# Pyramid-pooled attention on one core: earlier weights, turns of the identity, another order in the last batch, and six banks for the last projections

## The reference, cut to what matters

```python
# x: (8, 512, 64, 64) f32; qk_w: (256, 512); v_w: (512, 512); out_w: (512, 512)
qk  = relu(bn(einsum('bchw,oc->bohw', x, qk_w)))
val = relu(bn(einsum('bchw,oc->bohw', x, v_w)))
key    = psp(qk)                        # max pools to 1, 3x3, 6x6, 8x8: 110 cells
value  = psp(val).transpose(0, 2, 1)
query  = qk.reshape(B, 256, H * W).transpose(0, 2, 1)
scores = softmax(einsum('bnc,bcs->bns', query, key) * 256 ** -0.5)
y = einsum('bns,bsc->bnc', scores, value)      # back to (B, 512, H, W)
return x + bn(einsum('bchw,oc->bohw', y, out_w))
```

## Time and profile before

| what | value |
|---|---|
| median of 3 runs | 1314.9 us (1314.38 to 1315.77) |
| profiled execution, its own time | 1314.11 us |
| its span | 1312.4 us |
| TensorE busy | 1283.3 us, 98% of the span |
| GpSimd, VectorE, ScalarE busy | 951.9, 947.3, 688.7 us |
| granted clock of TensorE over the span | 0.997 |

### The profile page before, as it was taken

The page is one execution under the profiler, slowest core; times in us unless marked ns, Lnnn a source line. Parts: engine busy times, 40 slices in busy tenths (PEclk is TensorE's granted clock), DMA queues, the critical chain, the costliest instruction groups (busy, mean ns, idle before and its releaser), DMA issues.

```text
span 1312.4 us, 16789 instructions
## 1 busy us (share of the span) xinstructions
PE 1283.3 (98%) x5539; PEld 1036.1 (79%) x5539; DVE 947.3 (72%) x2171; ACT 688.7 (52%) x1017; POOL 951.9 (73%) x414
## 2 busy tenths in 40 slices
PE   7999999999999999999999999999999999999996
PEld 6777788887888878887888877888788887888875
DVE  6555677777777778778777777777867778876466
ACT  5333555644555654555654465654555647754421
POOL 1888988877878867887777786877778826765522
PEclk9999999999999999999999999999999999999998
DMA  6323356566676656676556676666667669995226
GB/s 225 113 97 113 112 177 213 196 217 223 210 240 217 198 187 232 211 238 224 182 207 232 222 232 204 205 200 233 206 219 239 211 205 365 331 308 201 96 97 257
DMA packets 134538, 272.20 MB, mean 207 GB/s; under 512 B 9227, under 2 KB 9267, under 8 KB 134451
## 3 DMA queue, kind: packets, MB, share of 16 engines
q1 hardware_dynamic: 133874, 270.07, 60.9%
q10 hardware_dynamic: 576, 1.05, 0.2%
HBM read 174.61 MB, written 96.47 MB: 207 GB/s over the span
## 4 chain that ended last, share of the span: by engine, by line
PE 79%; DVE 7%; POOL 7%; ACT 3%; DMA 2%; issue 2%; SPq 0%; DVEq 0%; ACTq 0%; POOLq 0%
PE conv_ps L690 16%; PE conv_ps L688 16%; PE conv_ps L692 16%; POOL xl L578 5%; PE out_ps L772 4%; PE out_ps L773 3%; PE out_ps L774 3%; PE conv_ps L673 3%; PE conv_ps L674 3%; PE conv_ps L672 3%; PE score_ps L746 2%; PE score_ps L745 2%; PE score_ps L747 2%; DVE row_max L1336 1%; DMA xa<-x 1%
## 5 line engine op out<-in xcount | busy, mean ns | idle before, releaser
L1336 DVE TENSOR_REDUCE row_max<-conv_ps 128x64 f32<-128x384 f32 (+2 forms) x576 | 284.5, 530 | 149.0 <-ACT q_out L1035 68.2
L578 POOL TENSOR_TENSOR xl<-xa,xh 128x1024 fp32r<-128x1024 f32 x108 | 258.0, 2418 | 84.5 <-ACT xh L964 84.5
L688 PE MATMUL conv_ps<-xh,sh 128*128 128x512 f32 x648 | 253.5, 391 | 3.8 <-POOL xl L578 1.8
L690 PE MATMUL conv_ps<-xh,sl 128*128 128x512 f32 x648 | 254.3, 393 | 0.0
L692 PE MATMUL conv_ps<-xl,sh 128*128 128x512 f32 x648 | 254.3, 392 | 0.0
L578 POOL TENSOR_TENSOR xl<-tt,xh 128x1024 fp32r<-128x1024 f32 x81 | 194.3, 2415 | 10.2 <-ACT xh L964 10.2
L688 PE MATMUL conv_ps<-xh,wh 128*128 128x512 f32 x486 | 190.2, 391 | 4.1 <-POOL xl L578 2.7
L692 PE MATMUL conv_ps<-xl,wh 128*128 128x512 f32 x486 | 190.7, 392 | 0.0
L690 PE MATMUL conv_ps<-xh,wl 128*128 128x512 f32 x486 | 190.6, 392 | 0.0
L972 ACT ACTIVATE conv_ps<-conv_ps 128x512 f32<-128x512 f32 x81 | 47.2, 583 | 253.6 <-PE conv_ps L692 252.9
L1476 DVE SCALAR_TENSOR_TENSOR xo<-out_ps,shift,xo 128x512 f32<-128x512 f32 x205 | 151.9, 745 | 34.5 <-DMA xo<-x 18.0
(11 more groups left out here) (227 smaller groups left out, 2527.7 us busy)
## 6 DMA issues: line engine op xcount, KB each, us to landing
xa<-x SPq DMA_DIRECT2D x148, 512.0 KB, 5.5
xo<-x SPq DMA_DIRECT2D x104, 512.0 KB, 4.3
out<-xo SPq DMA_DIRECT2D x104, 512.0 KB, 3.7
queries<-q_out SPq DMA_DIRECT2D x112, 256.0 KB, 2.5
q_in<-queries SPq DMA_DIRECT2D x50, 512.0 KB, 4.1
tt<-x SPq DMA_DIRECT2D x13, 512.0 KB, 5.5
out<-tt SPq DMA_DIRECT2D x13, 512.0 KB, 4.9
early<-queries SPq DMA_DIRECT2D x6, 512.0 KB, 7.8
```

The costliest lines, as they stand in the source:

```text
L578: nc.gpsimd.tensor_tensor(xl[:, b0:b1, :], raw, xh[:, b0:b1, :], ALU.subtract).then_inc(x_lo, 1)
L688: nc.tensor.matmul(out[:, :], hi[:, k, :], xh[:, b + k, :], start=first, stop=False, skip_group_check=True)
L690: nc.tensor.matmul(out[:, :], lo[:, k, :], xh[:, b + k, :], start=False, stop=False, skip_group_check=True)
L1336: last = nc.vector.tensor_reduce(row_max[:, c, n, :], src[:, r0_ * W:r1_ * W].rearrange("p (r w) -> p w r", w=W), AX.X, ALU.max)
```

## The change

The parts of the diff below belong to three places.

At the start: SyncE's queue gets the value weights 1 and 3 behind the two halves of x and before the key weights, ScalarE's queue keeps weights 0 and 2, and SyncE no longer waits before tile 1 of x. `scale_weights(1)` stands before the first split of x on VectorE. `keep_busy(n)` turns the identity n times into `conv_ps[2]`, whose content nothing reads: 5 times before the turn of the batch norm rows, 7 behind it, 10 between the first two turned weights and `conv(0, 0)`.

In the last image's values (s = 65 to 70): `scores(s - 8)` stands before `conv(s, 0)` instead of behind `conv(s, 1)`, and `sums(s - 8)` stands behind `conv(s, 1)` in the same s, where before it opened s + 1. GpSimd, ScalarE and VectorE follow: `split_q_lo` before `split_lo`, `exps` and `split_q_hi` before `split_hi`, `split_e_lo` before the pooling, `refine` and `normalise` before the pooling of group 2 and `split_p_lo` behind it.

At the very end: six banks in turn for the 32 projections, and nothing of tile 62's softmax is left there; tile 63's `sums` comes one tile earlier.

```diff
+        LAST_BANKS = [out_ps[0], *conv_ps[0:3], out_ps[1], score_ps]
         def out_bank(a, m):
-            return [out_ps[0], *conv_ps[0:3]][m] if a >= LAST else out_ps[m % 2]
+            return LAST_BANKS[(OC * (a - LAST) + m) % len(LAST_BANKS)] if a >= LAST else out_ps[m % 2]
@@ sync
+            for m in ORDER[2:VC]:
+                sp.dma_start(w_raw(m), v_w[m * P:(m + 1) * P, :]).then_inc(w_in[m], 16)
             sp.dma_start(qk_raw[:, :, :], qk_w.rearrange("(m p) c -> p m c", p=P)).then_inc(w_in[VC], 16)
-            sp.wait_ge(w_in[VC - 1], 16)
             load(1)
@@ gpsimd
-                if LAST < s < S:
+                if s < X - 1 and s not in (LAST, S):
                     split_q_lo(s - (NT - 1))
...
-                if s < X - 1 and not LAST < s < S:
+                if s in (LAST, S):
                     split_q_lo(s - (NT - 1))
@@ tensor
+            def keep_busy(n):
+                for _ in range(n):
+                    nc.tensor.transpose(conv_ps[2][:, 0:P], ident[:, :], ident[:, :])
             pe.wait_ge(ident_made, 2)
+            keep_busy(5)
             pe.wait_ge(bn_in, 16)
             nc.tensor.transpose(conv_ps[3][:, 0:4 * PAR], bn_rows[:, :], ident[0:4 * PAR, 0:4 * PAR]).then_inc(bn_turned, 1)
@@ project
-                if copied(a - 1, m):
-                    pe.wait_ge(y_copied, a - LAST)
-                else:
-                    wait(pe, out_added, added(a - 1, m) if a > LAST else OC * a + m - 1)
+                n = OC * (a - LAST) + m
+                if n >= len(LAST_BANKS):
+                    n -= len(LAST_BANKS)
+                    if copied(LAST + n // OC, n % OC):
+                        pe.wait_ge(y_copied, n // OC + 1)
+                    else:
+                        pe.wait_ge(out_added, added(LAST + n // OC, n % OC))
+                elif n < 0:
+                    wait(pe, out_added, OC * a + m - 1)
+                elif n == 0:
+                    pe.wait_ge(out_added, OC * LAST - 1)
+                elif n == 5:
+                    pe.wait_ge(p_lo, S - 1)
@@ tensor
+            keep_busy(7)
             turn_weights(0)
             turn_weights(1)
+            keep_busy(10)
...
             for s in range(S, X):
-                if s < X - 1:
+                if s <= S + 1:
                     sums(ap)
                 if s == S:
                     project(ap - 1, 2)
                     project(ap - 1, 3)
+                elif s < X - 1:
+                    scores(ac)
                 conv(s, 0)
                 conv(s, 1)
                 if s == S:
                     project(ap, 0)
                     project(ap, 1)
                 elif s < X - 1:
-                    scores(ac)
+                    sums(ac)
                 conv(s, 2)
...
-            sums(S - 2)
             for a in range(LAST, S):
                 for m in range(OC):
                     project(a, m)
-                if a == LAST + 2:
+                if a == LAST + 1:
                     sums(S - 1)
@@ scalar
-            for m in ORDER[0:VC]:
+            for m in ORDER[0:2]:
                 act.dma_start(w_raw(m), v_w[m * P:(m + 1) * P, :]).then_inc(w_in[m], 16)
...
+            for s in range(S + 1, X - 1):
+                a = s - NT
+                if s == S + 1:
+                    guess(a - 1)
+                exps(a)
+                split_q_hi(a + 1)
+                split_hi(s + 1, 0)
+                split_hi(s + 1, 1)
+                if s == S + 1:
+                    split_p_hi(a - 1)
+                guess(a)
+                split_p_hi(a)
...
             exps(S - 1)
-            guess(S - 2)
             copy_out(LAST)
-            split_p_hi(S - 2)
@@ vector
+            scale_weights(1)
             split_first_lo(0)
             weights_lo(0)
-            scale_weights(1)
             split_first_lo(1)
...
+                    if s < X - 1:
+                        split_e_lo(ac)
...
                 for c in range(VC):
+                    if c == 2 and S < s < X - 1:
+                        refine(ac)
+                        normalise(ac)
                     pool_tile_rows(s, c)
+                    if c == 2 and S < s < X - 1:
+                        split_p_lo(ac)
...
             add_outs(LAST)
             split_e_lo(S - 1)
-            refine(S - 2)
             add_outs(LAST + 1)
-            normalise(S - 2)
             add_outs(LAST + 2)
-            split_p_lo(S - 2)
+            refine(S - 1)
             add_outs(LAST + 3)
-            refine(S - 1)
             normalise(S - 1)
```

More of the change, by code:

```diff
@@ L1184, in _ @@
                 store_pair_q(s, 3)
-            for s in range(LAST, X):
+            for s in range(LAST, S + 1):
                 ap, ac = s - NT - 1, s - NT
-                if 0 <= ap < S - 2:
-                    guess(ap)
+                guess(ap)
                 if s == LAST + 1:
@@ L1200, in _ @@
                     split_q_hi(ac + 1)
-                if s + 1 < X:
-                    split_hi(s + 1, 0)
+                split_hi(s + 1, 0)
                 if s == LAST:
                     split_hi(s + 1, 1)
-                if 0 <= ap < S - 2:
-                    split_p_hi(ap)
+                split_p_hi(ap)
                 if s == LAST:
@@ L1211, in _ @@
                     finish_keys(ac // NT)
-                if LAST < s < X - 1:
+                if LAST < s:
                     split_hi(s + 1, 1)
@@ L1222, in _ @@
                     continue
-                if 0 <= ac < S - 1 and not LAST < s < S:
+                if s == S:
                     exps(ac)
-                if 0 <= ac + 1 < S and not LAST < s < S:
                     split_q_hi(ac + 1)
@@ L1676, in _ @@
                         add_out(ap, 2 * c - 1)
-                    if c == 2 and s < X - 1:
+                    if c == 2 and s == S:
                         split_e_lo(ac)
```

## The result

The changed kernel takes 1304.62 us (median of 4 runs, 1303.7 to 1305.68); the kernel before, measured with it, 1315.13 us (1314.38 to 1315.77). The ratio is 0.9921, with a 95% interval of 0.9905 to 0.9937: 10.5 us less. The profiled execution of the change took 1303.70 us, with a span of 1302.0 us.

A forecast was written before the change was run, and what follows sets the result against it. TensorE, busy 98% of the span, bounds the kernel; start -2.4 and tail -8.0 give -10.4 on 1314.1, 1303.7, plus 0.8 for the median: 1304.5 us. Range: about 1302.6, with 0.7 for the runs' spread, to 1308.2.

The forecast's parts named there:

- The start: Up to the first convolution's end: earlier scaling, reordered loads and turns gain 2.4 us, all kept to the end.
- the rise of the clock: TensorE at the start: upper clock level reached at 10.6 us at the latest, at the earliest by the convolution's start.
- The rule against the change: First convolution: by the skill's rule transposes do not bring the full clock, so the turns would not raise it.
- rival B: First convolution: turns do not raise the clock, only its own matmuls do; gain 0.7 instead of 2.4, 1306.2 us; chance 0.27.
- The last image: Last image's values: moved sums cost 0.5 us and one new wait for queries 0.3 us, 0.8 in all.
- The end: Last projections and stores: TensorE goes through without a stop, then stores bind at 373 GB/s; 8.8 us gained before subtracting 0.8.
- My other two estimates of this term: Span's end: 1304.5 by the old lag behind the last add, 1304.9 by the worse window's 353 GB/s, against 1303.6 taken.
- One of my own signs of being wrong: Projections over 26 us, stores more than 6 us behind the adds, or new waits in tiles 65 to 70.
- my sum of 22.9 us for the projections: Tail: the 32 projections and last sums, 98 matmuls, need 22.9 us at 0.234 us spacing, against 30.9 before.
- C: Tail: VectorE or the copies on ScalarE and GpSimd set the pace; 2.8 us missing, 1307.3 us; chance 0.14.
- D: Start: loads of one queue share bandwidth, second half of x lands near 14.5 us; 1310.6 us; chance 0.05.
- E: Tiles 65 to 70: TensorE waits in each for the queries' low part; slower, 1317.5 us or more; chance 0.03.

The follow-up runs named there:

- run 2: The changed kernel with loads, order of weight scaling and turns at the start as before, last image and end as in the change: 1307.87 us, ratio 0.9945.
- run 3: The changed kernel with four banks and the old waits for the last projections, as before: 1307.43 us, ratio 0.994.
- run 5: The changed kernel storing only the second half of the channels of tiles 56 to 62, output incomplete: 1301.81 us, ratio 0.9891.
- runs 3 and 4: Besides run 3, the kernel before with five banks in turn for the last projections and nothing else: 1312.12 us, ratio 0.9975.
- run 1: The changed kernel without its 22 turns of the identity: 1306.56 us, ratio 0.9939.
- run 9: The changed kernel with the second weight scaled behind the first low weight, as before: 1308.2 us, ratio 0.9947.
- run 6: The changed kernel with the last image stored in quarters of a tile, each as soon as it is added: 1303.57 us, ratio 0.9913.
- run 12: The changed kernel itself once more, for a second profile: 1304.87 us, ratio 0.9928.
- run 10: The changed kernel without the group of ten turns; the groups of 5 and 7 stay: 1306.58 us, ratio 0.9929.
- run 8: The changed kernel with all four value weights on ScalarE's queue and SyncE waiting for the last, as before: 1305.42 us, ratio 0.9928.
- run 7: The changed kernel with quarter-tile stores and low parts of the second and third combined weights made while tile 1 is pooled: 1304.15 us, ratio 0.9916.

## Why the prediction was right

The sum was -10.4 us on the profiled execution, and -10.4 was measured; the forecast of 1304.5 stands against 1304.62. The mechanisms were right, but that the number is met so closely is luck. Two of its terms were off and cancelled; the stretch between them, which differs among executions by up to 4.4 us, happened to be almost as long in both profiles (1166.5 and 1166.1 us).

*The start* was put at 2.4 and gave 3.1 to 3.6. The mechanism was right: second weight turned before 7 us, convolution at 8.73 at full clock, the second half of x in time, and the lead carried to tile 65 and beyond (run 2: 3.2 us). What was mis-sized is the rise of the clock, which I put at 10.6 at the latest, from the one row of before, 4.75 us of work without a stop. The six profiles with the change's start have it between before 5.6 and 9.35 us, and the convolution lost at most one matmul at the lower level. Why it comes earlier than by that row stays open. On average over these profiles the start gives about 2.7 us, so the term was nearer than this one pair of executions says. That the second lead is 3.6 and not 3.1 I ascribe to nothing: the stretch between differs by 4.4 us among the profiles of the study.

*The rule against the change*, in the Trainium skill, "TensorE: Matmul & The Clock Gate", section "Part 4: PE-mode transpose" (transposes don't bring the full clock), does not hold here. In run 3 the only work TensorE had done before 5.59 us were transposes, and the four at 5.59 took 0.66 us together instead of 1.12. The 0.27 that rival B got rested on it in part; no row of before could say better.

*The last image* cost 0.8 us as summed: 0.5 for the sums that moved (the gap ahead of the first projection, which they filled in part before, grew from 0.59 to 1.06), 0.3 for the one wait.

*The end* was put at 8.8 gross and gave 7.6. TensorE behaved as worked out: 31.7 us from first projection to last add became 23.9, without a wait or a low clock. The step that was too good is that the stores move 373 GB/s from the first to the last: 22.5 + 2.5 us from the first issue, against 1302.0 - 1275.92 = 26.1. The rate was there (363 to 383 in the good windows, so the 358 that the Trainium skill gives in "DMA: Bandwidth & Descriptors", section "Where 436 GB/s comes from", did not bind), but the two gaps at 1282 and 1285 took about 1.0 us together, one behind TensorE's pace and one behind VectorE's refinement. My other two estimates of this term, by the old lag and by the worse window, gave 7.9 and 7.5; I chose the best of three. One of my own signs of being wrong, stores more than 6 us behind the adds, was met by a hair (6.07); the other two were not. And 299 GB/s lies outside the 350 to 375 that I expected of every window. That the stores bind at all was right (run 5). I also did not part the end's mechanisms; runs 3 and 4 do in part. The moved softmax is worth more than the banks that I began with, and a third part, tile 56's single wait in place of one for each group (1.8 us of TensorE's time in run 3), is in my sum of 22.9 us for the projections without being named.

*The rivals.* B fell with run 1. C did not come about: VectorE's lag stayed inside the six banks, and even with four it cost only 0.3 us behind the first tile. D (a queue's loads side by side) shows nowhere: the second half of x had landed before 7.33. E did not come about; no tile from 66 to 70 has a wait.

## What to carry to other kernels

Look at what stands between the critical steps on the engines that free buffers. Here a copy queued behind an unrelated wait on ScalarE, and a softmax step between two adds on VectorE, cost more than too few banks did, and moving them to a stretch where these engines had room cost 0.8 us and gave 5.6. A wait that is stricter than the buffer needs is as dear: the one of tile 56 cost 1.8 us with all its banks free. So look for it before you add buffers. Work without use can be worth putting on TensorE where it waits anyway and a stream of matmuls follows, but it must be covered: uncovered, as in run 9, it delays what it was meant to speed up. When the last engine is no longer late, look at the stores: begin them with the first piece that is ready (1 us in run 6).

## What the runs showed of the hardware

- Transposes alone brought TensorE to its upper level: four turns in 0.66 us at 5.59 us in run 3, behind nothing but turns, where the same four took 1.12 us in run 12.
- The moment of the rise differs between executions of one program: before the ten turns in one profile of the change (1.25 us for them) and at their end in the other (2.23 us). In run 10 it came 5.3 to 6.0 us behind the first convolution's start, in run 8 4.4 to 4.8, and in the programs without turns 2.6 to 4.3.

The granted clock that the windows give is no help at the start. For the kernel before it reads so:

```profile
10.00:20.00 10.00, 10.00 (x44) 8.20 (x43) 5.91 (x12) 2.92 (x7) 0.00 (x0) 1.00 0.84 309
```

That is 1.00, while the matmuls up to 13.98 are 0.43 us apart. So at the start the spacing has to be read, and neither this column nor the slices of the page. At the end the same column does fall (0.66 in the earlier trace rows).

One more, of the queues: stores of 512 or 256 KB reached 363 to 385 GB/s in windows of 4 us (the change, and run 7's last). While they flowed at that rate, issuing the last four of 256 KB took SyncE 4.04 us, where the first two of 512 KB, with nothing in flight, took 0.90 together.
